# A selective state space block and a ternary feed-forward: B replicated by TensorE, sums of the weights paced by ScalarE's own reloads, and the work of a steady tile in another order

## The reference

```python
# xattn: a selective scan over ctx, gated by the normalised x
xin   = in_proj_w @ ctx.T                              # [512 channels, 512 positions] per batch
u     = silu(causal_conv4(xin) + conv_b)
dt, Bm, Cm = split(x_proj_w @ u, [16, 16, 16])         # 48 rows
delta = softplus(dt_proj_w @ dt + dt_proj_b)
state = state * exp(delta * A) + delta * u * Bm        # per channel 16 states, along the positions
y     = sum_n(state * Cm) + D * u
x     = x + tanh(g_xattn) * (y * silu(layernorm(x).T)).T
# ffn: three linear layers; activations rounded to 8 bits a row, weights to -1, 0, 1 times arctanh(mean |w|)
n     = layernorm(x)
h     = silu(bit(n, w1, g1)) * bit(n, w2, g2)          # [2048 rows, 2048]
out   = x + tanh(g_ffn) * bit(h, w3, g3)
# bit(v, w, g) = quant(g * rmsnorm(v)) @ ternary(w).T
```

## Time and profile before

| | us |
|---|---|
| three runs | 718.72, 718.19, 714.82 (median 718.19) |
| the profiled execution | 720.12 |
| its span, first to last instruction | 718.1 |
| mean granted clock of TensorE | 0.909 of full speed |

### The profile page before, as it was taken

One profiled execution on the slowest core, in us unless ns is written; L12 is line 12 of the kernel. 1 busy time (PEld: TensorE's weight loads), 2 busy tenths in 40 slices (PEclk: granted clock), 3 DMA queues, 4 the chain that ended last, 5 costly groups with the idle time before them and its releaser, 6 DMA issues.

```text
span 718.1 us, 8217 instructions
## 1 busy us (share of the span) xinstructions
PE 619.6 (86%) x2538; PEld 248.4 (35%) x2538; DVE 607.9 (85%) x620; ACT 558.4 (78%) x805; POOL 548.3 (76%) x316
## 2 busy tenths in 40 slices
PE   6736765999869999999989999998897979796997
PEld 3311221544343333334333434332333323233443
DVE  2979959899967899987989899999999989877665
ACT  3647885689679997896879997989698969557873
POOL 2055549987598989897889999999899897967732
PEclk9865887999879999989999999999897979798999
DMA  8599873548922122233411212154111111000000
GB/s 220 168 257 330 287 269 91 165 148 231 297 86 74 44 59 74 59 81 83 93 28 53 52 47 56 46 120 102 49 55 45 45 44 45 15 16 0 16 31 29
DMA packets 40570, 72.01 MB, mean 100 GB/s; under 512 B 10912, under 2 KB 13472, under 8 KB 38352
## 3 DMA queue, kind: packets, MB, share of 16 engines
q1 hardware_dynamic: 37312, 62.07, 30.7%
q10 hardware_dynamic: 3216, 9.44, 3.9%
HBM read 50.51 MB, written 4.46 MB: 77 GB/s over the span
## 4 chain that ended last, share of the span: by engine, by line
PE 44%; DVE 17%; POOL 16%; issue 7%; DMA 7%; ACT 6%; SPq 2%; DVEq 0%; POOLq 0%; ACTq 0%
PE ring L1519 13%; DVE hb L1138 8%; PE y_ps L1497 7%; PE ring L1606 6%; POOL hb L668 6%; DVE dbu_ps L1129 5%; PE du_ps L1484 4%; POOL up_sb L625 4%; PE ring L1569 3%; POOL h L632 3%; DMA dl_rep<-delta 3%; DMA bc_rep<-bc_scratch 2%; PE ring L1446 2%; PE ring L1465 2%; PE ring L1456 2%
## 5 line engine op out<-in xcount | busy, mean ns | idle before, releaser
L1138 DVE TENSOR_TENSOR_SCAN hb<-dA,dbu_ps 128x1024 f32<-128x1024 f32 x128 | 292.4, 2284 | 13.5 <-ACT dA L874 4.6
L668 POOL TENSOR_TENSOR hb<-hb,bc_rep 128x2048 f32<-128x2048 f32 x52 | 235.8, 4537 | 46.7 <-DVE hb L1138 38.8
L874 ACT ACTIVATE dA<-dl_rep,a_neg 128x511 f32<-128x511 f32 x252 | 160.9, 714 | 18.9 <-DMA dl_rep<-delta 18.7
L1129 DVE TENSOR_TENSOR dbu_ps<-du_ps,bc_rep 128x1024 f32<-128x1024 f32 x128 | 157.6, 1231 | 18.5 <-PE du_ps L1484 8.2
L1497 PE MATMUL y_ps<-hb,sel_s 128*32 128x512 f32 x512 | 125.7, 636 | 2.2 <-POOL hb L668 2.2
L1484 PE MATMUL du_ps<-du,sel_q 32*128 32x512 f32 x128 | 79.9, 706 | 46.9 <-DVE dbu_ps L1129 46.5
L632 POOL TENSOR_TENSOR h<-h,up_sb 128x1024 f32<-128x1024 f32 x24 | 56.5, 2353 | 19.8 <-ACT up_sb L892 19.3
L1606 PE MATMUL ring<-w3T,hT 128*128 128x512 fp8e4 x256 | 61.5, 387 | 1.5 <-ACT hT L959 1.1
L663 POOL TENSOR_TENSOR hb<-hb,bc_rep 128x1024 f32<-128x1024 f32 x22 | 51.8, 2357 | 11.9 <-DVE hb L1138 11.6
L1497 PEld LDWEIGHTS y_ps<-hb,sel_s 128*32 128x32 f32 x512 | 28.5, 116 | 87.2 <-issue 81.5
L625 POOL TENSOR_TENSOR up_sb<-h,g3b 128x1024 f32<-128x1024 f32 x24 | 56.4, 2373 | 0.1
(11 more groups left out here) (174 smaller groups left out, 950.6 us busy)
## 6 DMA issues: line engine op xcount, KB each, us to landing
dl_rep<-delta SPq DMA_DIRECT2D x252, 64.0 KB, 2.0
bc_rep<-bc_scratch SPq DMA_DIRECT2D x32, 256.0 KB, 5.2
h<-in_L_ffn_w_dram SPq DMA_DIRECT2D x5, 1024.0 KB, 8.5
x<-in_L_ffn_w_dram SPq DMA_DIRECT2D x5, 1024.0 KB, 7.3
up_sb<-in_L_ffn_w_dram SPq DMA_DIRECT2D x5, 1024.0 KB, 7.9
xt<-in_x_dram SPq DMA_DIRECT2D x16, 256.0 KB, 3.1
out_dram<-x SPq DMA_DIRECT2D x16, 256.0 KB, 2.0
h<-in_L_ffn_w_dram ACTq DMA_DIRECT2D x3, 1024.0 KB, 6.1
```

Of the source, the lines that this page charges most:

```text
L668: g.tensor_tensor(hb[:, s % 4, :, :], hb[:, s % 4, :, :], c_rep(s // 16), ALU.mult)\
L874: ins = a.activation(dA[:, s % 2, i, 1:L], dl[:, 1:L], ACT.Exp, scale=a_neg[:, s % 16, i:i + 1])
L1129: v.tensor_tensor(dbu_ps[:, :, :], du_ps[:, :].unsqueeze(1).to_broadcast([P, 2, L]), b_rep(b)[:, 2 * half:2 * half + 2, :], ALU.mult).then ...
L1138: v.tensor_tensor_scan(hb[:, s % 4, 2 * half:2 * half + 2, :].rearrange("p a l -> p (a l)"), dA[:, s % 2, 2 * half:2 * half + 2, :].rearra ...
```

## The change

Parts, as the diff has them:

1. B of batch 0: TensorE replicates it with four products (`replicate_b`, two ahead of the delta broadcast, two behind `bcast_du(0)`), VectorE copies each out (`copy_b`); `load_b(0)` goes. Batches 1 to 3 keep the DMA.
2. ScalarE's tanh of the gates moves from its first place to before the last silu of the start.
3. Chunks: the first three are loaded ahead of `store_bc(0)`; two sums a step in steps 0 to 5; ScalarE issues the reload right behind each sum, on its own DMA queue.
4. The z statistics: eight ahead of the first scan, eight spread over tile 0; `z_affine` in two parts.
5. g1 and g2 are loaded at steps 9 and 10, g3 at step 18, behind C of batch 1, with a semaphore of its own.
6. Convolutions: none in the last tile of a batch; the first tile of a batch does two (in tile 4 both late, in tile 8 one early and one late; late means behind the transposed yz). The diagonal taps are made once, ahead. Fillers before the hidden transposes only where no late convolution is and et is not 3.
7. GpSimd in step 0: gain of the first half ahead of the second `times_up`, then the whole row affine (for f % 4 != 0), then the second gain, then `hidden_rms`. It also makes the dequantising scales, in step 2.
8. VectorE: first hidden maximum between product and scan of step 1; `hidden_scales` ahead of the last scan of step 1; `add_scan` between product and scan of step 2 (for et != 0); `row_var`, `row_bias` (f % 4 != 0) and `dequant_scales` gone.

Small buffers are aliased (`sel_s` becomes columns of `sel_q`, `ones` and the z statistics lie in `hT`) to make room for `diag_w` of four tiles.

```diff
 
-def conv_first(k):
-
-    return k >= LEARLY and k % ET != ET - 1
+def early_convs(k):
+
+    if k < LEARLY or k % ET == ET - 1:
+        return []
+    m = k + AHEAD - (k % ET == 0)
+    return [m] if m < KQ else []
+
+
+def late_convs(k):
+
+    if k < 1 or k % ET == ET - 1:
+        return []
+    if k % ET == 0:
+        m = [k + AHEAD] if k >= LEARLY else [k + AHEAD - 1, k + AHEAD]
+    else:
+        m = [k + AHEAD] if k < LEARLY else []
+    return [i for i in m if i < KQ]
...
-                if k >= 1 and k + AHEAD < KQ:
-                    pair.insert(0 if conv_first(k) else len(pair), ("conv", k + AHEAD))
-                jobs += pair
+                jobs += [("conv", m) for m in early_convs(k)]
+                if k >= 1:
+                    jobs.append(("yzT", k - 1))
+                jobs += [("conv", m) for m in late_convs(k)]
...
 
-    first = (0, 0, 2, 4, 7, 10, WCH)
+    first = (0, 2, 4, 6, 8, 10, WCH)
     return range(first[s], first[s + 1]) if s + 1 < len(first) else []
...
             def load_chunk(j):
-                if WB <= j:
-                    sp.wait_ge(w_abs, j - WB + 1)
                 sp.dma_start(chunk_buf(j), chunk_src(j % WCH)).then_inc(chunk_ld(j)[0], 16)
 
             def store_out(ft):
@@ -503,11 +529,11 @@
             sp.wait_ge(ctxT_done, 2)
             sp.dma_start(ctx_nat(1), ctx_in[1].rearrange("(t p) d -> p t d", p=P)).then_inc(ld_ctx, 16)
             load_xt(0)
+            for j in range(WB):
+                load_chunk(j)
             store_bc(0)
-            load_b(0)
             bcast_delta(1)
             load_c(0)
-            load_chunk(0)
...
+                    if s == TERN_AT + 2:
+                        sp.wait_ge(at_series, 1)
+                        sp.dma_start(g1b[:, :], g1.partition_broadcast(P)).then_inc(ld_g, 16)
+                    if s == TERN_AT + 3:
+                        sp.dma_start(g2b[:, :], g2.partition_broadcast(P)).then_inc(ld_g, 16)
+                    if s == Q * LAG_F + 2:
+                        sp.wait_ge(z_read, KQ)
+                        sp.dma_start(g3b[:, :], g3.partition_broadcast(P)).then_inc(ld_g3, 16)
...
+            def row_affine(ft):
+
+                if ft >= 4:
+                    pool.wait_ge(xn_done, ft - 3)
+                pool.wait_ge(row_square, row_sums(ft))
+                col = fsc[:, ft % 4, :]
+                link(g.tensor_scalar(col[:, 0:1], fmv[:, ft % 4, 1:2], (1.0 + RMS_EPS) / D, RMS_EPS * LN_EPS,
+                                     ALU.mult, ALU.add))
+                link(g.tensor_tensor(col[:, 1:2], col[:, 0:1], half_neg[:, :], ALU.pow))
+                g.tensor_tensor(col[:, 2:3], fmv[:, ft % 4, 0:1], col[:, 1:2], ALU.mult).then_inc(fbias, 1)
+
+            def dequant_scales(ft):
+
+                pool.wait_ge(a_scale, ft + 1)
+                if ft == 0:
+                    pool.wait_ge(alpha_done, 1)
+                if ft >= 4:
+                    pool.wait_ge(silu_done, 4 * (ft - 3))
+                    pool.wait_ge(up_done, 4 * (ft - 3))
+                g.tensor_tensor(deq[:, ft % 4, :], am[:, :], alpha[:, 0:2], ALU.mult).then_inc(deq_done, 2)
 
...
-            z_affine()
+            pool.wait_ge(masks, 1)
+            pool.wait_ge(ld_small, 64)
+            for et in range(ET):
+                diag_taps(et)
+            z_affine(0)
             for k in range(KQ):
                 f, gt = k - LAG_F, k - LAG_G
                 for q in range(Q):
                     s = Q * k + q
                     if s >= 1:
                         times_c(s - 1)
+                    if s == Q:
+                        z_affine(1)
                     if TERN_AT <= s < TERN_AT + WCH:
                         tern(s - TERN_AT)
                     if s == TERN_AT:
                         alpha_small()
                     if q == 0 and gt >= 0:
                         times_up(gt, 0)
+                        h_gain(gt, 0)
                         times_up(gt, 1)
                         if f % ET:
-                            row_rstd(f)
-                        h_gain(gt, 0)
+                            row_affine(f)
                         h_gain(gt, 1)
-                    if q == 2 and k + 1 + AHEAD < KQ:
-                        diag_taps(k + 1 + AHEAD)
+                        hidden_rms(gt)
+                    if q == 2 and f >= 0:
+                        dequant_scales(f)
                     if q == 1:
-                        if gt >= 0:
-                            hidden_rms(gt)
                         if k + 1 < KQ:
                             mul_du(k + 1)
...
@@ -914,8 +961,11 @@
             a.activation(a_neg[:, :, :], a_neg[:, :, :], ACT.Exp).then_inc(a_done, 1)
             for et in range(ET):
                 tap(et)
-            for et in range(ET):
+            for et in range(ET - 1):
                 silu_u(et)
+            act.wait_ge(ld_gate, 32)
+            a.activation(gates[:, :], gates[:, :], ACT.Tanh).then_inc(gate_done, 1)
+            silu_u(ET - 1)
             step_sizes(0)
             exps(0)
             ctx_evac(1)
...
                     if q == 1:
                         if sizes_due(k):
                             step_sizes(k + 1)
-                        if k + AHEAD < KQ and conv_first(k):
-                            conv_evac(k + AHEAD)
+                        for m in early_convs(k):
+                            conv_evac(m)
                         if f >= 0 and f % ET:
                             normalise(f)
                         if g >= 0:
                             quant_hidden(g)
-                        if 1 <= k < KQ - AHEAD and not conv_first(k):
-                            conv_evac(k + AHEAD)
+                        for m in late_convs(k):
+                            conv_evac(m)
                     if q == 2 and f >= 0:
                         quant(f)
                     if q == 3 and et == 2 and b + 2 < B:
@@ -1019,8 +1069,9 @@
                         silu_z(k)
                         if k == 0:
                             silu_u(ET)
-                        if k + AHEAD < KQ:
-                            silu_u(k + AHEAD)
+                            silu_u(AHEAD)
+                        for m in early_convs(k) + late_convs(k):
+                            silu_u(m)
                         if f >= 0:
                             for c in range(4):
                                 if k == KQ - 1 and c == 3:
@@ -1033,6 +1084,8 @@
                         act.wait_ge(*chunk_ld(c))
                         a.activation(chunk_buf(c), chunk_buf(c), ACT.Abs, accum_out=wsum[:, c:c + 1])\
                          .then_inc(w_abs, 1)
+                        act.wait_ge(w_abs, c + 1)
+                        a.dma_start(chunk_buf(c + WB), chunk_src((c + WB) % WCH)).then_inc(chunk_ld(c + WB)[0], 16)
                     if s == TERN_AT - 1:
                         act.wait_ge(w_scale, 1)
...
-            z_row_stats(1)
-            z_row_stats(2)
+            for k in range(KQ // 2):
+                z_row_stats(k)
+            for k in range(KQ // 2):
+                z_row_aggr(k)
 
             dve.wait_ge(delta_done, 1)
             dve.wait_ge(u_done, 1)
             v.tensor_tensor(du[:, 0, :], delta[:, 0, :], u[:, 0, :], ALU.mult).then_inc(du_done, 1)
-            z_row_stats(3)
+            copy_b(0)
+            copy_b(1)
 
...
@@ -1313,38 +1377,50 @@
                 for q in range(Q):
                     s = Q * k + q
                     add_input(s, 0)
+                    if s == 0:
+                        copy_b(2)
+                        copy_b(3)
+                    if k == 0 and q >= 1:
+                        z_row_stats(KQ // 2 + 2 * q - 2)
                     if q == 1:
                         if k == 0:
                             convolve(AHEAD)
+                        if g >= 0:
+                            hidden_max(g, 0)
                     if q == 2:
                         if f >= 0 and f % ET == 0:
                             row_bias(f)
+                        if k >= 1 and et:
+                            add_scan(k - 1)
                     scan(s, 0)
                     add_input(s, 1)
                     if q == 3 and g >= 0:
                         output(g)
                     if q == 1 and g >= 0:
-                        hidden_max(g, 0)
                         top = hidden_max(g, 1)
-                    if q == 0 and f >= 0 and f % ET:
-                        row_var(f)
-                    if q == 1 and f >= 0 and f % ET:
-                        row_bias(f)
                     if q == 1 and k >= 1:
                         gated_y(k - 1)
+                    if q == 1 and g >= 0:
+                        after(top)
+                        hidden_scales(g)
                     if q == 2:
                         if f >= 0:
                             quant_scales(f)
+                    if k == 0:
+                        if q >= 1:
```

(30 more changed lines are left out.)

134 lines of the change are left out of this document (67 added, 67 removed).

## The result

The changed kernel takes 711.86 us in the median of 6 runs (710.35 to 713.44), the kernel before 716.03 on the same chip; the ratio is 0.9938 with a 95% interval of 0.9909 to 0.9966. Run again later, beside two variants, it was 711.81 with a ratio of 0.9917 (0.9884 to 0.9949). So the change gains 4 to 7 us where 19 were forecast. The profiled execution took 710.35 us, 9.8 less than the profiled one of before (720.12). That one lay 1 to 4 us above the medians of the kernel before in all rounds (716.03 to 718.74); the forecast had corrected for 1.9.

A forecast was written before the change was run, and what follows sets the result against it. No engine is full over the span, but VectorE bounds the steady tiles, with GpSimd close behind. Terms -1 - 0.4 - 0.5 - 14.3 - 5.5 + 3 = -18.7 take the profiled 720.12 to 701.4, less 1.9: forecast 699 us, range 687 to 711.

The forecast's parts named there:

- start, tiles 0 and 1: First scan 0.5 us earlier, tile 0 +4.7 covered by the weight-sum wait: -1 at tile 2, bounds -5 and +4.
- tiles 2 and 3: The output addition moves into the gap between a product and its scan, 0.2 us each: -0.4.
- tile 4: Wait for C goes, row maxima come 2 us later, du wait shrinks about 2.5: net -0.5, bounds -6 and +3.
- steady tiles and clock: Tiles 5 to 15: -14.3 us as hidden-scale waits go; TensorE's half clock after lost fillers and convolution: +3.
- tile 7: Its half-clock convolution and ten filler products go, leaving VectorE's length: -5.5 us, bounds -6 and -3.
- tail: The 79 us after the last tile are left alone: 0.
- the bad side: At the start, half clock doubles TensorE's product times under the replication; the start is up to 2 us later.
- the bound of +3: Tile 4's upper bound: +3 us if the convolutions run at half clock, 5.6 us each.
- The clock's +3: Tiles 7, 11, 15 lose fillers, TensorE idles before hidden transposes: +1 us a tile, bounds 0 and +12.
- The first: Rival: early part falls out badly, or GpSimd takes half the steady gain; 707 us, chance 0.23.
- The second: Rival: tile 4 really loses its stall, -6 instead of -0.5, and no clock is lost; 691 us, chance 0.2.
- The third and fourth: Rivals: half clock from tiles 7, 8, 11, 15's hidden transposes, 740 us, 0.07; GpSimd's power still late, 713, 0.08.

The follow-up runs named there:

- e1: Changed kernel with all sixteen row statistics of z and their aggregates ahead of the first scan; median 4 to 5 us below e2, e3 and e4, intervals overlapping the changed kernel's.
- e4: Changed kernel with B of the first batch element by DMA again, first three weight chunks behind it; median -0.8 us from its base, inside the intervals.
- e2: Changed kernel with convolution 8 back in tile 3, only 9 in tile 4; tile 4 from 47.0 to 44.0 us, the whole did not move.
- e3: Changed kernel with the weight-chunk reloads issued by SyncE again instead of ScalarE; no difference to the whole.
- i3: The changed kernel itself, run again; 711.81 us, ratio 0.9917 to the kernel before.
- f1: Kernel before with only the steady tile's reordering on VectorE and GpSimd; tiles 5 to 15 took 400.0 us against 413.7, as fast as the whole change or faster.
- g3: f1 with ScalarE's tanh moved from the head of its queue to among the first SiLUs; median 709.1 us, no gain shown.
- f3: e1 with B of the first batch element by DMA again, first three weight chunks ahead of it; median +1.3 us from its base, inside the intervals.
- f2: e1 with GpSimd's two first-row gains in tile 4 behind its multiplication by C of step 1; tile 4 from 45.8 to 44.8 us, intervals overlap.
- g1: e1 with ScalarE's normalisation of each batch element's first row ahead of the late convolutions' evacuation; median 701.6 us, 5.5 faster than e1 on another chip.
- i2: The kernel of g1 again, beside i3 on one chip; 701.38 us against the changed kernel's 711.81.
- g2: e1 with all convolutions and filler matmuls where the kernel before had them; median 7 us above e1's.
- h2: g1 with the loads of gains g1, g2 and g3 where they were before; median 1.2 us higher, inside the intervals.
- i1: g1 with du and the state sum ahead of the last weight transposes in tile 4; tile 4 39.1 us and tile 5 42.5, against 40.4 and 36.8 in i2.
- f4: e1 with the last two weight sums on ScalarE ahead of the step sizes; 4.4 us slower than e1 in the median, another chip, intervals just overlap.

## Why the prediction was wrong

The forecast's terms beside what the two profiled executions show (us):

```
term                        forecast   measured
start, tiles 0 and 1          -1.0       +2.0    step that failed
tiles 2 and 3                 -0.4       +2.0    missed
tile 4                        -0.5       +3.1    step that failed
steady tiles and clock       -11.3      -10.5
tile 7                        -5.5       -5.2    size right, cause half wrong
tail                           0         -0.9    by two effects that cancel
```

**Start and weight sums.** The failed step is "Six of them stand between a product and its scan, a gap that is free ... Net +4.7 for tile 0. What covers it is the wait of 6.0 for the weight sums". Tile 0 grew by 6.8: 4.3 us go with the statistics (e1), 2.6 with the replication and its wait for du (e4). (The prediction's own figures, 4.9 + 0.8 - 6 x 0.2, make 4.5 and not 4.7.) It was not covered: the wait for the sums fell only from 6.0 to 4.2, since the same delay reached VectorE's gated product (91.13), TensorE's convolution (95.52 to 99.1) and, behind it, the sums (end at 104.2, not 101). I had followed that chain and then taken ScalarE's sum less as enough to break it. Tiles 0 and 1 together show this whatever the start of an execution was: 78.1 us in the changed kernel (77.5 to 78.9 in e2, e3 and i3), 73.9 before and 73.0 in f1. e1 takes the statistics away and has tile 2 start at 114.75, 0.7 before the kernel before. That is near the forecast's -1, but no proof of it, since the forecast had the statistics in tile 0.

The first scan came 2.2 us earlier where 0.5 was forecast. That is within its bounds, and in part luck: the 3.1 us that the tanh's move gave at the step-size products were in no term (it was counted as 0), and the half clock that I had named as the bad side took most of them back. In the whole neither the tanh (g3) nor the replication (e4, f3) shows a gain.

**Tiles 2 and 3.** TensorE's granted clock there was 0.86 and 0.95, against 0.88 and 1.00. In e2 the same convolution took 5.64 us in tile 3 where it took 3.59 before. I had no term for the clock before tile 5. The new start is not needed for this loss: f1, with the start, sums and loads of before, takes 69.9 us for tiles 2 and 3 where the kernel before takes 66.1, with a clock of 0.91 in tile 3. The only part of f1 at work before tile 4 is the output addition one step later, for which the forecast had -0.4. Whether it is the cause was not tested, and there is one profiled execution of each kernel: this stays open.

**Tile 4.** The maxima came at T+29.4, as forecast to 0.4 us. The failed step is the next one: the wait for du at the end "hangs on TensorE's own queue and shrinks by about 2.5". It grew by 1.1, and that is the whole miss: steps 0 to 2 of the tile took 1.9 us more, as forecast, and the last one 1.2 more. The convolutions were not the reason, as the bound of +3 had it; they ran near full clock (7.68 us for sixteen products). GpSimd, which stood 10.6 us for the normalised row, came late with its product, the rounding of the last chunk and thus TensorE's transposes (f2: with the product ahead of the gains, that wait is 2.7). The mistake is in the method: I listed what waits for the normalisation on VectorE, and not what is queued behind it on GpSimd. g1 shows the price of the order on ScalarE that I had read correctly and taken as given: tile 4 is 3.7 us shorter than in e1, and 5.4 in i2.

**Steady tiles, tile 7, clock.** The 13.8 us of the earlier trace rows went as forecast, with 2.9 us of waits for a hidden maximum in tiles 5 to 14 (1.4 before). f1 shows 3.3 of tile 7's 5.2 us as the reordering's; the regrouping gives 2 there and takes 2.5 in tile 8, where I had said 2 (g1 gives 2.3 back, so what costs in tile 8 is the evacuations' place ahead of the normalisation). The clock's +3 did not show as such: from tile 8 to 15 the granted clock was 0.93 before and 0.92 now; only in tile 11 it fell, from 0.95 to 0.90, and that tile gained 0.5 us where tile 10 gained 1.5. So about 1 of the 3 us is seen, and the steady tiles gave some 11.5 and not 14.3: VectorE waits 2.5 us for the row maxima of tile 8, and 2.0 and 1.7 us more than before for hidden maxima and du. The sum of both terms was right to 0.8 us in part by luck.

**Tail.** 0 was near by two effects that cancel: the reordering makes it 1.7 us longer (f1), the regrouping 2.6 shorter (g2 against e1).

**The rivals.** The first came nearest, at 707: half clock under the replication, statistics not covered and tile 4 at +3 all occurred. The early part was worse than it had (+7.1 where the forecast had -1.9), and of the steady part's gain most stayed. The second fell by h2: the stall was worth 1 to 3 us in its tile, not 6. The third and fourth did not occur. The Trainium skill's rule (DMA: Bandwidth & Descriptors, section "Issuing engines are not separate DMA queues"), weighed in the prediction, says that all issuing engines share the same 16 DMA engines and only issue time is saved. The landings did not stay at 8 us as the prediction had it by that rule: the broadcasts of delta between 50 and 75 us landed in 5.4 us (8.2 in the earlier trace rows), and in 8.9 with the reloads back on SyncE (e3). The whole moved as it would by that rule, not at all.

**The base.** The prediction took 1.9 us off a profiled 720.12; the later medians of the kernel before (716 to 719) would have asked for up to 4. That accounts for part of the difference between 9.8 us in the profiled executions and 4 to 7 in the medians.

## What to carry to other kernels

When an edit delays an instruction, list what is queued behind it on every engine that waits, not only on the one whose wait you are removing: here GpSimd stood 10.6 us in its queue, and its product, a rounding and TensorE's transposes came late behind it. A wait covers an added cost only if its releaser does not hang on the delayed engine itself; follow the releaser back once around. And before moving work out of one tile, ask which engine is full in the tile that receives it: e2, g2, h2 and i1 each moved 1 to 6 us into a neighbouring tile or step and gained nothing.

## What the runs showed of the hardware

A tiny VectorE operation can be held for a whole GpSimd operation: L1311 in f4, on 128x3 elements, took 4.43 us beside a multiplication of 4.50 us, against 0.17 for the same operation in e1, where GpSimd stood still. Not every one is: in the changed kernel an operation on 128x1 elements at 216.22 took 0.15 us beside the same kind of multiplication. The Trainium skill (SBUF — State Buffer, section "SBUF: two separate sides") says that the two share one pair of ports under an exclusive lock, held for the whole instruction by the one that starts first, when VectorE's operation is in a two-port mode or has two inputs in SBUF. The times in f4 agree: the multiplication started 0.1 us ahead. Which mode VectorE was in no trace here shows.

The start varies between executions of the same instructions. g1 and its repeat i2 have their first scan at 41.81 and 44.92 us, and e1, whose instructions up to there are the same, at 39.34. Stretch 20 to 30 us, i2 first, then e1:

```profile
20.00:30.00 10.00, 7.10 (x11) 1.65 (x9) 9.82 (x17) 5.92 (x9) 0.00 (x0) 0.66 1.06 391
```

```profile
20.00:30.00 10.00, 7.54 (x14) 2.24 (x15) 9.89 (x17) 6.34 (x10) 0.00 (x0) 0.83 1.05 392
```

The granted clock was 0.66 in the one and 0.83 in the other; g1 had 0.83 as well, so this stretch alone does not explain the difference. A spread of 5.6 us is as much as most edits here are worth, so a first scan of one execution is no measure of an edit at the start; medians over rounds and lengths of tiles are.
